# One state of a selective scan leaves the transposed path: its product with C moves to GpSimd

## The reference

```python
xn = layernorm(x)
xc, z = split(xn @ in_proj_w)                    # 1024 channels each
xc = silu(conv4(xc))                             # along the sequence
dt, B, C = rmsnorm'ed parts of xc @ x_proj_w     # 32, 16, 16 wide
dt = softplus(dt @ dt_proj_w + dt_bias)
for t:                                           # per channel d and state n
    h[d, n] = exp(dt[t, d] * A[d, n]) * h[d, n] + dt[t, d] * B[t, n] * xc[t, d]
    y[t, d] = sum_n h[d, n] * C[t, n]
s = ((y + D * xc) * silu(z)) @ out_proj_w
g = silu(down(silu(gate(xn)) * up(xn)))          # quantised weights with a low-rank part
out = x + s * g
```

## Time and profile before

| | us |
|---|---|
| median of 3 runs | 1173.33 |
| the 3 runs | 1170.23, 1173.33, 1177.11 |
| the profiled execution: its own time | 1170.76 |
| its span in the trace | 1168.9 |
| PE busy | 1114.6 (95%) |
| DVE busy | 947.9 (81%) |
| POOL busy | 734.4 (63%) |
| ACT busy | 644.6 (55%) |

### The profile page before, as it was taken

One profiled execution on the slowest core, in us unless ns is written; L12 is line 12 of the kernel. 1 busy time (PEld: TensorE's weight loads), 2 busy tenths in 40 slices (PEclk: granted clock), 3 DMA queues, 4 the chain that ended last, 5 costly groups with the idle time before them and its releaser, 6 DMA issues.

```text
span 1168.9 us, 12511 instructions
## 1 busy us (share of the span) xinstructions
PE 1114.6 (95%) x4430; PEld 595.2 (51%) x4430; DVE 947.9 (81%) x789; ACT 644.6 (55%) x816; POOL 734.4 (63%) x406
## 2 busy tenths in 40 slices
PE   5998999999999999999999899999999999999998
PEld 3443455555545555555444345555555555555543
DVE  4897899999789999985325379999988899999630
ACT  3225577777717777760022357777874477787200
POOL 2000899999537999980410048999973599999211
PEclk9998999999999999999999999999999999999999
DMA  8663389999914999988511125999994289999841
GB/s 252 207 219 115 105 204 222 216 246 239 247 49 125 226 225 223 250 179 285 200 36 36 45 78 147 218 232 223 240 226 143 102 191 231 207 256 213 251 175 45
DMA packets 61778, 214.26 MB, mean 183 GB/s; under 512 B 6666, under 2 KB 6794, under 8 KB 61204
## 3 DMA queue, kind: packets, MB, share of 16 engines
q0 software_dynamic: 16128, 88.09, 38.4%
q1 hardware_dynamic: 44004, 119.70, 30.6%
q10 hardware_dynamic: 1584, 5.68, 1.2%
HBM read 102.52 MB, written 22.85 MB: 107 GB/s over the span
## 4 chain that ended last, share of the span: by engine, by line
PE 48%; POOL 24%; DVE 14%; issue 8%; DMA 3%; ACT 2%; POOLq 0%; DVEq 0%; SPq 0%; ACTq 0%
POOL ub L594 20%; PE psM L966 11%; PE psM L1026 9%; PE psA L806 9%; DVE hb L1189 8%; PE psT L944 7%; PE psM L956 4%; POOL yT L604 4%; PE psM L836 4%; DVE xc L1053 2%; DMA yT<-yc 2%; PE psA L916 1%; DVE hid L1053 1%; DMA w_ts<-w_in_dram 1%; PE psM L860 1%
## 5 line engine op out<-in xcount | busy, mean ns | idle before, releaser
L594 POOL TENSOR_TENSOR ub<-dtx,bn 128x1024 f32<-128x1024 f32 x256 | 645.8, 2570 | 287.8 <-DMA bn<-ss_rows_scratch 187.5
L1189 DVE TENSOR_TENSOR_SCAN hb<-psA,ub 128x1024 f32<-128x1024 f32 x256 | 579.7, 2279 | 10.6 <-POOL ub L594 4.8
L699 ACT ACTIVATE psA<-dt,cc 128x1024 f32<-128x1024 f32 x256 | 285.9, 1118 | 129.4 <-DVE hb L1189 128.7
L836 PE MATMUL psM<-xnT,w_ts 128*126 128x512 f32 x704 | 329.0, 598 | 4.4 <-DVE th L1053 4.2
L944 PEld LDWEIGHTS psT<-ident,hb 128*128 128x128 f32 x2048 | 233.4, 140 | 179.0 <-issue 87.1
L944 PE MATMUL psT<-ident,hb 128*128 128x128 f32 x2048 | 281.7, 276 | 16.7 <-DVE yT L1053 14.8
L720 ACT ACTIVATE yc<-psT,ssm 128x512 f32<-128x512 f32 x336 | 217.4, 678 | 51.4 <-PE psT L944 49.2
L836 PEld LDWEIGHTS psM<-xnT,w_ts 128*126 128x126 f32 x704 | 122.5, 190 | 113.0 <-issue 113.0
L966 PE MATMUL psM<-w_dn,hid 126*128 126x512 f32 x352 | 164.3, 594 | 0.0
L1053 DVE SCALAR_TENSOR_TENSOR yT<-psT,ssm,yT 128x512 f32<-128x512 f32 x144 | 104.9, 735 | 31.6 <-PE psT L944 30.3
L956 PE MATMUL psM<-xnT,w_ts 128*128 128x512 f32 x256 | 119.6, 594 | 2.2 <-DMA w_ts<-w_in_dram 2.2
(11 more groups left out here) (82 smaller groups left out, 530.3 us busy)
## 6 DMA issues: line engine op xcount, KB each, us to landing
yT<-yc POOLq DMA_DIRECT2D x112, 768.0 KB, 8.8
bn<-ss_rows_scratch SPq DMA_DIRECT2D x64, 512.0 KB, 7.0
w_ts<-w_gu_scratch SPq DMA_DIRECT2D x44, 504.0 KB, 4.7
w_ts<-w_in_dram SPq DMA_DIRECT2D x32, 256.0 KB, 7.2
hb<-z_scratch SPq DMA_DIRECT2D x16, 512.0 KB, 8.0
w_gu_scratch<-hid ACTq DMA_DIRECT2D x11, 504.0 KB, 4.2
yT<-x_dram SPq DMA_DIRECT2D x8, 512.0 KB, 9.0
z_scratch<-th SPq DMA_DIRECT2D x16, 256.0 KB, 8.1
```

The costliest lines, as they stand in the source:

```text
L594: pool.tensor_tensor(ub[:, i % 2, :], dtx[:, i, :], bn[:, t, :], ALU.mult).then_inc(s_u, 1)
L699: act.activation(psA[:, i % 2, :], dt[:, i, :], ACT.Exp, scale=negA[:, h * DH + i, bass.ds(n, 1)]).then_inc(s_a, 1)
L836: mm = pe.matmul(psM[0:IM, gu, :], w_ts[:, t, at:at + IM], xnT[:, k, h * CH:(h + 1) * CH], start=(k == 0), stop=(k == HK - 1))
L1189: dve.tensor_tensor_scan(hb[:, t * DH + i, :], psA[:, i % 2, :], ub[:, i % 2, :], 0.0, ALU.mult, ALU.add).then_inc(s_scan, 1)
```

## The change

The last state of each half is no longer turned. `turn`, `add_y` and `scale_y` now run over ROWS = 15 states. In place of the sixteenth state's turns, POOL multiplies each of its four scanned tiles in place by C's row 15 (`times_c`), which SP loads, broadcast, into `bn[:, 0]` (the new "C" in SP_LATE); for that C's rows are turned and stored beside B's at the start of a sequence. DVE's new `add_skip` forms `xc = D*xc + hb` from these tiles, and `add_rows`, after `turn_back`, adds `psT` to it. The first B row of the next half goes into the same buffer as C's row, and so waits for all four products (`s_hc`). POOL issues the last addition to `yT` behind three of the products.

The 76 (70) steps of z and down are spread anew: two in each of the 28 slots that still turn, and the rest (20 in a sequence's second half, 14 in the first) over the last four.

```diff
+ROWS = NS - 1
+STEP = 2
 def steps_of(p, h):
     steps = STEPS if h else STEPS[:-REST]
-    return steps[len(steps) * p // QUARTERS:len(steps) * (p + 1) // QUARTERS]
+    turned = QUARTERS - 4
+    if p < turned:
+        return steps[STEP * p:STEP * (p + 1)]
+    left, at = len(steps) - STEP * turned, p - turned
+    return steps[STEP * turned + left * at // 4:STEP * turned + left * (at + 1) // 4]
...
-           ("B", 14), ("z", 3, 1), ("G", 0), ("w",), ("B", 15), ("d", 0, 0), ("d", 1, 0), ("W",), ("N", 0), ("back",),
-           ("G", 1),
-           ("d", 2, 0), ("N", 1), ("d", 3, 0)]
+           ("B", 14), ("z", 3, 1), ("G", 0), ("w",), ("B", 15), ("C",), ("d", 0, 0), ("W",), ("back",), ("d", 1, 0),
+           ("N", 0), ("G", 1), ("d", 2, 0), ("N", 1), ("d", 3, 0)]
...
                     def load_b(n, t, h=h):
                         sp.wait_ge(s_u, unit(b, h, n, 0) + 4)
+                        if n == 0 and b + h > 0:
+                            sp.wait_ge(s_hc, blk(b, h, 0))
...
+                        elif what[0] == "C":
+                            sp.wait_ge(s_u, unit(b, h, NS - 1, 0) + 8)
+                            sp.dma_start(bn[:, 0, :], ss_rows[b, E - 1:E, :].to_broadcast([P, L])).then_inc(s_crow, 16)
...
-                    gather_y(NS - 2, 1)
+                    def times_c(i):
+
+                        pool.wait_ge(s_scan, unit(b, h, NS - 1, i) + 3)
+                        pool.tensor_tensor(hb[:, DH + i, :], hb[:, DH + i, :], bn[:, 0, :], ALU.mult).then_inc(s_hc, 1)
+
+                    pool.wait_ge(s_crow, 16 * (b * HALVES + h + 1))
+                    for i in range(DH - 1):
+                        times_c(i)
+                    gather_y(ROWS - 1, 1)
+                    times_c(DH - 1)
...
                     def add_skip(i):
 
+                        k, m = blk(b, h, i), h * DH + i
+                        dve.wait_ge(s_hc, k + 1)
+                        stt(xc[:, m, :], xc[:, m, :], cc[:, m, DP:DP + 1], hb[:, DH + i, :], ALU.mult,
+                            ALU.add).then_inc(s_ym, 1)
+
+                    def add_rows(i):
+
                         k, m = blk(b, h - 1, i), (h - 1) * DH + i
                         dve.wait_ge(s_yb, k + 1)
-                        stt(xc[:, m, :], xc[:, m, :], cc[:, m, DP:DP + 1], psT_row, ALU.mult, ALU.add).then_inc(s_ybr, 1)
+                        dve.wait_ge(s_ym, k + 1)
+                        dve.tensor_tensor(xc[:, m, :], xc[:, m, :], psT_row, ALU.add).then_inc(s_ybr, 1)
...
-                        turn(n, n % 2, y_order(n)[2 * q])
-                        turn(n, n % 2, y_order(n)[2 * q + 1])
+                        if n < ROWS:
+                            turn(n, n % 2, Y_ORDER[2 * q])
+                            turn(n, n % 2, Y_ORDER[2 * q + 1])
...
+                        if n == ROWS:
+                            add_skip(q)
```

More of the change, by code:

```diff
@@ L103, with y_pos @@
 Y_ORDER = [2, 0, 3, 4, 5, 1, 6, 7]
-def y_order(n):
-    return list(range(TB)) if n == NS - 1 else Y_ORDER
-def y_pos(n, tb):
-    return y_order(n).index(tb)
-TD_HALF = (NS - 1) * YD + TB
-TC_HALF = (NS - 1) * YA
+def y_pos(tb):
+    return Y_ORDER.index(tb)
+TD_HALF = ROWS * YD
+TC_HALF = ROWS * YA
 SCRATCH = 2048
@@ L283, in build @@
         s_ybr = sem("s_ybr")
+        s_crow = sem("s_crow")
+        s_hc = sem("s_hc")
+        s_ym = sem("s_ym")
         s_zl = [sem(f"s_zl{i}") for i in range(DH)]
@@ L305, in t_group, with by_dve @@
         def t_group(b, h, n, tb):
-            return b * T_DVE + h * (NS * TB) + n * TB + tb
+            return b * T_DVE + h * (ROWS * TB) + n * TB + tb
         def summed(b, h, n, tb):
-            at = n * YD + tb if n < NS - 1 else (NS - 1) * YD + y_pos(n, tb)
-            return (b * HALVES + h) * TD_HALF + at
-        def by_dve(n, tb):
-            return n == NS - 1 or tb < YD
+            return (b * HALVES + h) * TD_HALF + n * YD + tb
+        def by_dve(tb):
+            return tb < YD
         def ring(n, e):
@@ L561, in _ @@
                     sp.wait_ge(s_tfd, t_group(b, HALVES, 0, 0))
+                    sp.wait_ge(s_ym, blk(b, HALVES, 0))
                     load_small()
@@ L719, in scale_y @@
                             to = yc[:, ring(n, e), a, :]
-                        act.activation(to, psT[:, y_pos(n, tb) % 2, :], ACT.Copy,
+                        act.activation(to, psT[:, y_pos(tb) % 2, :], ACT.Copy,
                                        scale=ssm[:, tb, R + NS + n:R + NS + n + 1]).then_inc(s_tcp, 1)
@@ L773, in _ @@
                             for tb in Y_ORDER[2 * i:2 * i + 2]:
-                                if not by_dve(n, tb):
+                                if not by_dve(tb):
                                     scale_y(n, tb)
@@ L785, in _ @@
                         for tb in Y_ORDER[2 * (p % 4):2 * (p % 4) + 2]:
-                            if not by_dve(LATE + p // 4, tb):
+                            if LATE + p // 4 < ROWS and not by_dve(tb):
                                 scale_y(LATE + p // 4, tb)
@@ L900, in turn_b_rows @@
                     for a in range(TB):
-                        mm = pe.transpose(psT[0:NS, a // JD, a % JD * P:(a % JD + 1) * P], ssm[:, a, R:R + NS],
+                        mm = pe.transpose(psT[0:2 * NS, a // JD, a % JD * P:(a % JD + 1) * P], ssm[:, a, R:E],
                                           ident[:, :])
@@ L922, in turn_back @@
                         pe.wait_ge(s_tdve, summed(b, h, 0, 0))
+                        for e in range(2):
+                            pe.wait_ge(s_yacc[e], gathered(b, h - 1, ROWS - 1))
                         pe.wait_ge(s_ybr, blk(b, h - 1, i) + 1)
@@ L929, in turn @@
                     def turn(n, t, tb):
-                        at = y_pos(n, tb)
+                        at = y_pos(tb)
                         if at == 0:
@@ L937, in turn @@
                             n0 = n if at > 1 else n - 1
-                            tb0 = y_order(n0)[at - 2]
-                            if by_dve(n0, tb0):
+                            tb0 = Y_ORDER[at - 2]
+                            if by_dve(tb0):
                                 pe.wait_ge(s_tdve, summed(b, h, n0, tb0) + 1)
@@ L1184, in scan @@
                             dve.wait_ge(s_y, blk(b, h - 1, i) + 2)
+                        if h and n == 1:
+                            dve.wait_ge(s_ym, blk(b, h - 1, i) + 1)
                         dve.wait_ge(s_a, unit(b, h, n, i) + 1)
@@ L1234, in _ @@
                         for i in range(DH):
-                            add_skip(i)
+                            add_rows(i)
                             times_z(i)
@@ L1256, in _ @@
                     else:
-                        add_skip(0)
+                        add_rows(0)
                         times_z(0)
                         drive(1, 3)
-                        add_skip(1)
+                        add_rows(1)
                         scan(0, 0, 0)
                         times_z(1)
-                        add_skip(2)
+                        add_rows(2)
                         silu_late(0, "d", JD - 1, 0)
@@ L1266, in _ @@
                         times_z(2)
-                        add_skip(3)
+                        add_rows(3)
                         silu_gate(0, 0)
@@ L1286, in _ @@
                             scan(n + 1, 1 - n % 2, q)
-                        if by_dve(n, y_order(n)[2 * q]):
-                            add_y(n, y_order(n)[2 * q])
+                        if n < ROWS and by_dve(Y_ORDER[2 * q]):
+                            add_y(n, Y_ORDER[2 * q])
                         if p:
@@ L1291, in _ @@
                                 silu_late(h, *what)
-                        if by_dve(n, y_order(n)[2 * q + 1]):
-                            add_y(n, y_order(n)[2 * q + 1])
+                        if n < ROWS and by_dve(Y_ORDER[2 * q + 1]):
+                            add_y(n, Y_ORDER[2 * q + 1])
                         if p == 0:
                             hidden(IT - 1, (IT - 1) % 2)
-                        if h + 1 < HALVES and n == NS - 1 and q > 0:
+                        if n == ROWS:
+                            add_skip(q)
+                        if h + 1 < HALVES and n == ROWS and q > 0:
                             drive(h + 1, q - 1)
```

16 lines of the change are left out of this document (8 added, 8 removed).

## The result

| | before | after |
|---|---|---|
| median, us | 1172.38 (6 runs, 1170.23 to 1177.11) | 1185.41 (6 runs, 1183.18 to 1187.34) |
| the profiled execution: its own time / span | 1170.76 / 1168.9 | 1187.34 / 1185.7 |
| PE, DVE, POOL, ACT busy, us | 1114.6, 947.9, 734.4, 644.6 | 1111.7, 978.0, 774.8, 641.4 |

The changed kernel is slower: ratio 1.0106, 95% interval 1.0083 to 1.0128.

The account below looks back on a forecast made before the run. The ring of input, decay and scan, DVE fullest, paces the seven late states, PE the tail; 4.2 + 2.0 + 1.4 = +7.6 us, from 1172.0 to 1179.6 us, range 1172 to 1188.

Parts of the forecast that it names:

- Second halves, +4.2: Moved steps make tails after S (state 15's first scan) longer, S comes earlier: +2.0 and +2.2 us.
- First halves, +2.0: Ring gain, late B row and shorter tail in a sequence's first halves: -0.2 and +2.2 us.
- The wait for B's row 15: In first halves the last z tile is stored a slot later, so the row comes late by 1.9 and 2.9 us.
- the -0.7 of each tail: First halves, from S to the first turn back: 27.1 us against 27.8, fourteen steps taking 12.0.
- the 0.0 of the ring: Input, decay and scan from state 8 to S take 79.8 us, so half three gains nothing.
- Meetings at the next half's start, +1.4: GpSimd inputs hold up VectorE there: 0.7 us for each of two passages, bounds 0 and 2 x 1.85.
- Products and last addition hidden, 0: In the tails, the addition to yT lands at S + 24.5, 2.6 us or more before PE waits for it.
- the third rival: The last addition lands late, at S + 30, and the turn back waits 2 to 3 us: 1187.6 us, chance 0.15.
- VectorE's multiply-adds, 0: Four of 1.2 us each in the tail end while PE works off its steps, so they cost nothing.
- B's row in time, no meetings: Rival: z stores land early and inputs fall between DVE's instructions, +1.4 us, 1173.4; chance 0.27.
- PE paces the late states: Rival: the seven late states follow PE, not the ring, so its 14 us come off: 1158 us, chance 0.06.
- come off whole by themselves: The last state's turns, 3.5 us of PE a half behind S, 14 over four halves, would be saved entirely.

Follow-up runs that it names:

- Run 1: The kernel before with only its late steps spread anew and its 16 turned states kept, no products and no C row: 1196.61 us, ratio 1.0177.
- run 3: The changed kernel with B's row 15 moved ahead of the next half's weights G and w in SP's late order: 1181.37 us, ratio 1.0059.
- run 4: The changed kernel with the next half's first B row in the other buffer, issued ahead of the load of z: 1182.92 us, ratio 1.0067.
- Run 2: The changed kernel with the old even spread of the z and down steps: 1186.52 us, ratio 1.0093.
- run 5: The changed kernel with the old even spread, and the last addition to yT issued behind the first product: 1174.92 us, ratio 1.0022.
- run 6: Run 5 with the edits of run 3 (B's row 15 earlier) and run 4 (other row buffer): 1176.89 us, ratio 1.0023.
- run 9: Run 6 with the four products on VectorE, each ahead of its multiply-add, none on GpSimd: 1176.05 us, ratio 1.0026.
- run 11: Run 9 with the last state's product, multiply-add and drive ahead of the late tile in VectorE's stream: 1174.82 us, ratio 1.0020.

## Why the prediction was right, and where a term was too small

*Direction and cause were as forecast:* slower, 1179.6 forecast and 1185.4 measured, inside 1172 to 1188. The size was not: the sum of +7.6 stands against +13.0 between the medians. The terms below are read from the profiled executions, which lie 16.6 apart (the one before 1.6 under its median, the changed one 1.9 over), so 3.6 us of what they show is the difference between single executions.

*Second halves, +4.2:* measured 4.9. S came 0.75 and 0.55 us earlier, tails 28.21 and 27.96 for 28.05. Run 1 shows the mechanism by itself, and run 3's trace gives 2.3 and 2.8 again.

*First halves, +2.0:* measured 5.4. The wait for B's row 15 was there, and against run 3, where the row is in time (79.94 and 80.42 us from state 8 to S), it cost 2.9 and 2.5 us, for 1.9 and 2.9. What failed is the -0.7 of each tail (-0.2 and +0.9), and in half three the 0.0 of the ring (80.42 for 79.82). The fourteen steps took 12.8 us in half one's tail and not 12.0: beside the products for dt a step takes 0.91, not 0.86. And in half three PE, which had stood idle for 2.3 us behind the late row, ran at a granted clock of 0.56, near the lower of its two levels, for the next 3.9 us:

```profile
875.22:879.12 3.90, 3.90 (x9) 2.05 (x10) 3.88 (x2) 2.87 (x4) 3.74 (x2) 0.56 1.01 202
```

```profile
876.13 3.15 PE L988 MATMUL psM<-w_dn,hid 126*128 126x512 f32 x4
```

(1.88 at full clock). Without the wait, in run 3, that tail took 27.44 and not 28.72, at a granted clock of 1.00. After the same wait in half one of the changed kernel the clock stayed at 1.00. How late the row comes is no constant either: in run 4, with the same order up to it, it was late in half one alone.

*Meetings at the next half's start, +1.4:* measured 5.2, and 6.5 in run 3 (passages of 9.45 and 8.93); this is the term that was sized too small. The mechanism is the one forecast, with the bound of 3.7 for a passage nearly reached (3.3). I counted one meeting in two or three; GpSimd's two inputs stand right behind each other, so that VectorE met one with each of two instructions.

*Products and last addition hidden, 0:* right, by 0.3 us in half one, and not by the 2.6 forecast; that is luck. The addition was issued at S + 15.0 to 15.2 (forecast 15.7) but landed 11.6 to 12.4 us later, the slow landing of the third rival. With 12.3 the forecast's own sum gives S + 28.0, past its first halves' turn back at S + 27.1; the products ended 0.7 us sooner and the tails were 0.5 us longer. Run 2, where it decides, shows the addition holding the turn back at S + 27.3 to 27.7.

*VectorE's multiply-adds, 0:* right for the time, by other means. The page "SBUF — State Buffer" of the Trainium skill, section "Who interferes with whom", calls the port pair an exclusive lock, held for a whole instruction; worked out from that and a product's 2.35 us, an estimate, one such meeting costs at most 2.35 us. The trace has one that cost 7.4 (8.7 for 1.27) over nearly three products. The measurement decides; it did no harm, since PE worked until S + 28.

*The rivals.* "B's row in time, no meetings" falls on both waits. "PE paces the late states" falls: with less PE work they kept the ring's pace, 79.9 to 80.4 from state 8 to S (second halves of run 1, all halves of run 3).

*Where the turns' 14 us are.* The prediction said that they would come off whole by themselves, and run 5 shows that, up to the turn back. What it did not see is what stands next to PE: VectorE with its products, drives and multiply-adds (from S to the next first scan, no variant came below 32.96 us, before 33.75), and in second halves the last down tile: issued anywhere from S + 22.9 to S + 29.8, it landed at S + 31.1 to 34.4 before, after, and in each run with products whose trace was read. The loads of z and the output weights, issued from S + 14 on in all of them, are under way then, and SP's transfers landed in the order of issue, the last store 0.6 us behind the one ahead of it each time; run 1, where nothing was under way ahead of it, is the exception (2.0 us). That points to what stands ahead of it in SP's order as what holds it. No run placed those loads elsewhere, so it is not shown by an experiment, nor that the 14 us would then stay off.

## What to carry to other kernels

Before taking work off the engine that is busy throughout, look for what ends just behind it: here VectorE and a store with its way back were within one or two microseconds, so 14 us of TensorE were worth nothing in any arrangement tried. Work that a ring hides is free where it is, and full price once moved behind the ring. And GpSimd instructions right behind each other, beside a VectorE instruction with two SBUF inputs, may count as one long wait: four products did in every half, two inputs in the passage did not.

## What the runs showed of the hardware

- Beside GpSimd's back-to-back products a VectorE multiply-add took 8.7 us (1.27 alone), over GpSimd's second, third and fourth product; VectorE did not get in between two of them. Between two inputs of GpSimd, as close to each other (2.31 us from start to start, like the products), it did (half one, 326.12). With a gap on GpSimd (run 6, half one, between the first product and the second) one took 1.28.
- One accumulating transfer of 768 KB into `yT` landed after 7.2 us where it was issued ahead of the loads of z (run 5, half two) and after 11.6 to 12.4 where four loads of 512 KB stood beside it.
- A store of 256 KB took 4.7, 7.6 and 8.7 us when it was issued at S + 26.4, 23.9 and 22.9: it landed at S + 31.1 to 31.55 each time (half four, before and runs 9 and 11), 0.6 us behind the store issued ahead of it on SP. With that one landed already it took 2.0 (run 1).
- After 2.3 to 2.9 us without work the granted clock was 0.56 for 3.9 us in one place, 0.63 for 4.4 in another (run 9, 1125.62) and 0.50 for 4.3 in a third (run 4, 298.98), and 1.00 in a fourth.
